# Cumulative logs of the gates kept in DRAM by batch and head instead of by tile

## What is computed

```python
log_f = jax.nn.log_sigmoid(x @ Wf.T + delta)
lf = jnp.cumsum(log_f.reshape(b, nc, C, H).transpose(1, 0, 3, 2), axis=-1)   # C = 128
def step(S, inputs):
    qb, kb, vb, lb = inputs
    o_inter = jnp.einsum('bhid,bhde->bhie', qb * jnp.exp(lb)[..., None], S)
    A = jnp.einsum('bhid,bhjd->bhij', qb, kb)
    diff = jnp.where(mask, lb[..., :, None] - lb[..., None, :], -jnp.inf)
    A = A * jnp.exp(diff)
    ...
```

## Time and profile before

| | |
|---|---|
| median of three runs | 893.77 us |
| profiled execution | 893.34 us |
| its span, first to last instruction | 891.6 us |
| TensorE matmul, busy | 800.4 us, 90% |
| DVE / ACT / GpSimd, busy | 566.5 / 498.7 / 429.0 us |
| mean granted TensorE clock | 0.952 of full |
| SP's DMA queue: packets, MB | 119904, 145.00 |
| all DMA | 132847 packets, 163.89 MB, mean 184 GB/s |

### The profile page before, as it was taken

One profiled execution on the slowest core, in us unless ns is written; L12 is line 12 of the kernel. 1 busy time (PEld: TensorE's weight loads), 2 busy tenths in 40 slices (PEclk: granted clock), 3 DMA queues, 4 the chain that ended last, 5 costly groups with the idle time before them and its releaser, 6 DMA issues.

```text
span 891.6 us, 15824 instructions
## 1 busy us (share of the span) xinstructions
PE 800.4 (90%) x5648; PEld 682.0 (76%) x5648; DVE 566.5 (64%) x1027; ACT 498.7 (56%) x1165; POOL 429.0 (48%) x383
## 2 busy tenths in 40 slices
PE   1665799999999999999999999999999999999930
PEld 1443578888888888888888888888888888888830
DVE  5685455657855775557665766568656766556575
ACT  4654755566546664665556645665566545654431
POOL 5647641656245642566255815563357525470230
PEclk9965699999999999999999999999999999999975
DMA  8756796658667775678576766676667767663947
GB/s 284 283 166 157 206 343 221 159 152 186 194 157 159 188 195 143 150 183 202 154 160 181 156 219 142 164 187 193 157 140 193 195 157 210 162 134 117 277 106 221
DMA packets 132847, 163.89 MB, mean 184 GB/s; under 512 B 11808, under 2 KB 102432, under 8 KB 132640
## 3 DMA queue, kind: packets, MB, share of 16 engines
q1 hardware_dynamic: 119904, 145.00, 55.6%
q0 software_dynamic: 12288, 16.79, 12.1%
q10 hardware_dynamic: 576, 1.09, 0.3%
HBM read 117.48 MB, written 45.35 MB: 183 GB/s over the span
## 4 chain that ended last, share of the span: by engine, by line
PE 64%; DVE 8%; POOL 7%; ACT 5%; issue 5%; DMA 5%; SPq 1%; another core or an unknown queue 1%; DVEq 0%; ACTq 0%; POOLq 0%
PE g_ps L1408 16%; PE y_ps L1434 15%; PE up_ps L1408 15%; PE a_ps L1374 3%; PE o_ps L1398 3%; DMA qk_dram<-qk_r 3%; PE m_ps L1326 3%; PE m_ps L1356 2%; POOL w_r L803 2%; PE m_ps L1334 2%; POOL ffn_dram L833 2%; PE m_ps L1351 1%; POOL xg L821 1%; DMA w_raw<-w_experts 1%; ACT dec_both L971 1%
## 5 line engine op out<-in xcount | busy, mean ns | idle before, releaser
L1434 PE MATMUL y_ps<-w_r,hid_r 128*128 128x256 f32 x1536 | 205.5, 283 | 1.6 <-DVE hid_r L1292 1.6
L1408 PE MATMUL up_ps<-xgt,w_r 128*128 128x512 f32 x768 | 203.8, 400 | 0.0
L1408 PE MATMUL g_ps<-xgt,w_r 128*128 128x512 f32 x768 | 201.6, 398 | 1.0 <-DVE sg L1278 1.0
L1434 PEld LDWEIGHTS y_ps<-w_r,hid_r 128*128 128x128 f32 x1536 | 192.9, 190 | 3.1 <-DVE hid_r L1292 2.3
L1278 DVE SCALAR_TENSOR_TENSOR sg<-sg,g_ps 128x512 f32<-128x512 f32 x128 | 87.6, 685 | 169.2 <-ACT sg L1062 162.5
L803 POOL TENSOR_TENSOR w_r<-w_raw,w_r 128x768 fp32r<-128x768 f32 x64 | 122.3, 1912 | 101.5 <-ACT w_r L991 101.2
L1408 PEld LDWEIGHTS up_ps<-xgt,w_r 128*128 128x128 f32 x768 | 138.2, 188 | 25.9
L1408 PEld LDWEIGHTS g_ps<-xgt,w_r 128*128 128x128 f32 x768 | 135.5, 189 | 24.2 <-DVE sg L1278 0.8
L1062 ACT ACTIVATE sg<-g_ps 128x512 f32<-128x512 f32 x128 | 76.4, 597 | 125.7 <-PE g_ps L1408 121.7
L833 POOL DMA_INDIRECT ffn_dram<-y_sb,idx_all x64 | 105.0, 1640 | 74.7 <-DVE y_sb L1206 58.9
L798 POOL TENSOR_SCALAR_AFFINE_SELECT lb_row<-lb_row 128x1024 f32<-128x1024 f32 x64 | 78.2, 1232 | 95.5 <-DMA lb_row<-lb_tiles 95.4
(11 more groups left out here) (234 smaller groups left out, 950.5 us busy)
## 6 DMA issues: line engine op xcount, KB each, us to landing
lb_row<-lb_tiles SPq DMA_DIRECT2D x64, 512.0 KB, 4.5
w_raw<-w_experts SPq DMA_DIRECT2D x64, 384.0 KB
qk_dram<-qk_r SPq DMA_DIRECT2D x32, 512.0 KB, 4.4
k_st<-qk_dram SPq DMA_DIRECT2D x96, 128.0 KB, 3.3
arena<-qk_dram SPq DMA_DIRECT2D x192, 64.0 KB, 3.4
x_all<-x SPq DMA_DIRECT2D x8, 512.0 KB, 10.3
xn_dram<-xn SPq DMA_DIRECT2D x8, 512.0 KB, 5.5
e_row<-lb_tiles SPq DMA_DIRECT2D x64, 64.0 KB
```

The source lines that it names most:

```text
L1408: mm = pe.matmul(bank[:, :], w_r[:, m, a, at:at + P], xgt[:, b, k, half * 512:(half + 1) * 512], start=(j == 0 and k == 0), stop=(j == len ...
L1434: mm = pe.matmul(y_ps[:, j, :], hid_r[p][:, a, j * P:(j + 1) * P], w_r[:, m, b, DOWN:DOWN + D], start=(m == 0 and q == 0 and j % 2 == 0), ...
```

## The change

The tensor becomes `lb_rows` [batch, head, tile of the batch, token] instead of `lb_tiles` [tile, head, token]. So the 512 tokens of a head in a batch lie in one piece of 2 KB, and the 8 heads of one tile lie 2 KB apart in pieces of 512 bytes, where they were one piece of 4 KB. `load_rows` reads the 4 tiles of 8 heads in one transfer (2 for 8 in each batch); `load_lb` keeps its one transfer; `store_lb` needs one for each batch (8 in all, 2 before), and the waits on `d_out` follow.

```diff
-    lb_tiles = nc.dram_tensor("lb_tiles", [NT, H, P], F32, kind="Internal").ap()
+    lb_rows = nc.dram_tensor("lb_rows", [B, H, TPB, P], F32, kind="Internal").ap()
...
                     for kk in range(KD):
-                        for c in range(TPB):
-                            sp.dma_start(e_row[:, kk, c * P:(c + 1) * P],
-                                         lb_tiles[b * TPB + c, kk * HH:(kk + 1) * HH, :].unsqueeze(1)
-                                         .broadcast_to([HH, HD, P])).then_inc(row_in, 16)
+                        sp.dma_start(e_row[:, kk, :], lb_rows[b, kk * HH:(kk + 1) * HH, :, :].rearrange("h c n -> h (c n)")
+                                     .unsqueeze(1).broadcast_to([HH, HD, N])).then_inc(row_in, 16)
 
                 def load_lb(n):
                     if n >= 2:
                         sp.wait_ge(e_done, 2 * n - 2)
-                    sp.dma_start(lb_row[n % 2][:, :, :], lb_tiles[n // 2, n % 2 * HH:(n % 2 + 1) * HH, :].unsqueeze(0)
+                    b, c = n // 2 // TPB, n // 2 % TPB
+                    sp.dma_start(lb_row[n % 2][:, :, :], lb_rows[b, n % 2 * HH:(n % 2 + 1) * HH, c, :].unsqueeze(0)
                                  .broadcast_to([P, HH, P])).then_inc(lb_in[n % 2], 16)
...
                 def store_lb(p):
                     sp.wait_ge(lb_turned, 2 * p + 2)
-                    sp.dma_start(lb_tiles.rearrange("(g t) h n -> (t h) g n", g=TPB)[:, GROUPS[p], :], lbt[p])\
-                      .then_inc(d_out, 16)
+                    for g in range(GROUPS[p].start, GROUPS[p].stop):
+                        for half in range(2):
+                            sp.dma_start(lb_rows[2 * g + half, :, :, :].rearrange("h c n -> c h n"),
+                                         lbt[p][half * TPB * H:(half + 1) * TPB * H, g - GROUPS[p].start, :])\
+                              .then_inc(d_out, 16)
...
-                sp.wait_ge(d_out, 16)
+                sp.wait_ge(d_out, 16 * 2)
...
-                        pool.wait_ge(d_out, 32)
+                        pool.wait_ge(d_out, 16 * B)
...
-                    act.wait_ge(row_in, 16 * KD * TPB * (b + 1))
+                    act.wait_ge(row_in, 16 * KD * (b + 1))
```

More of the change, by code:

```diff
@@ L108, in build @@
                   head_rows, delta_row, logits, turned, xt_stored, y_sb, attn_w, wo_r, arena, fixed)
-        mixed(nc, stage_of(makers), x, out, xn_dram, xt_dram, qk_dram, lb_tiles, s_dram, ffn_dram, w_experts, d_out,
+        mixed(nc, stage_of(makers), x, out, xn_dram, xt_dram, qk_dram, lb_rows, s_dram, ffn_dram, w_experts, d_out,
               ident, tri, ones, head_rows, delta_row, logits, qs0, qs1, e_row, xg, small, y_sb, xt_stored, dec_more, aff_t, top_val, top_at,
@@ L449, in top_step, with mixed @@
         dve.match_replace(aff_t[:, :], top_val[:, at], aff_t[:, :], -1.0).then_inc(topk, 1)
-def mixed(nc, stage, x, out, xn_dram, xt_dram, qk_dram, lb_tiles, s_dram, ffn_dram, w_experts, d_out, ident, tri, ones,
+def mixed(nc, stage, x, out, xn_dram, xt_dram, qk_dram, lb_rows, s_dram, ffn_dram, w_experts, d_out, ident, tri, ones,
           head_rows, delta_row, logits, qs0, qs1, e_row, xg, small, y_sb, xt_stored, dec_more, aff_t, top_val, top_at, neg_lb, exp_rest, exp_tot,
```

## The result

The changed kernel took 897.06 us (median of 11 runs, 10 of them between 895.2 and 899.3) beside 893.86 us for the kernel before, measured with it: ratio 1.004, interval 1.0029 to 1.0051, so +3.2 us. A second measurement (the tenth experiment) gave 897.18 beside 892.86, ratio 1.0053 (1.0038 to 1.0068). The change makes the kernel slower by 0.4 to 0.5%, at or just over the 0.3% that the prediction took as the bound of no change.

What follows compares the result with a forecast made beforehand. TensorE, busy 90% of the span, was taken as the bound, with transfers setting the end only before 141 us. Start +1.6 us, SP's time, stores and steady part zero: 893.34 + 1.6 = 894.9, 895.4 against the median; range 890.5 to 901.

Steps and rivals of the forecast that it cites:

- The packets: SP's DMA queue: some 170400 packets for 119904, and its share up by some 4 points.
- The start: To about 141 us: `lb_row` loads delay two weight loads and a `qk_dram` store by 0.50, 0.10, 1.00: +1.6 us.
- A load costs 0.50 us more: Each `lb_row` load at a full queue: 1.76 us in 512-byte pieces for 1.26 in 4 KB pieces.
- the upper bound of +1.46: Most an `lb_row` load could cost more, if it ran at 193 GB/s like the q loads: 2.72 us.
- The dear packet: Rival, 20%: `lb_row` loads run like q loads at 193 GB/s; +5.6 us at the start, nothing per batch, 899.4 us.
- SP's time: SP's issues: fewer `e_row` issues free 3.7 us per batch, hidden by waiting for GpSimd's weight halves; cost zero.
- That rival: 14%: SP's freed time at 68.11 us shortens the chain's wait at 80.09 us; 891.6 or 889.5 us.
- The stores: Stores of the logs, eight for two: some 0.4 us delay and 2.6 us of SP, both covered; zero.
- The steady part: After about 141 us: 3.6 us more queue time per batch, hidden by slack; zero, period still 95.1 us.
- both places that the prediction named: Steady part: second `qk_dram` store with 3.2 us of slack, mask of `lb_row` with 3.7; both hide the added cost.
- the rival of the tight place: 6%: loads costing over 3.2 us more make the second `qk_dram` store late in seven batches; some 920 us.
- No price at all: Rival, 10%: short pieces run as fast as long ones, or the compiler joins them; -0.5 to 0, 893.5 us.

Runs made afterwards that it cites:

- the tenth experiment: The changed kernel, unaltered, run again on one chip with the kernel before and three variants: 897.18 us, ratio 1.0053.
- the seventh experiment: The changed kernel with `e_row` read in eight transfers again, from the new layout: 896.39 us, ratio 1.0062 to the kernel before.
- the rows alone: Kernel before with both layouts stored; `e_row` read in two transfers from the new one, `lb_row` in 4 KB pieces from the old: 891.84 us, 0.9995.
- The experiment with eight loads of 64: Kernel before with logs stored twice; only the first eight `lb_row` loads read 512-byte pieces 2 KB apart: 896.96 us, ratio 1.0056.
- the burst: Kernel before with logs stored twice, 48 loads appended, short pieces at several distances: 281 GB/s at 1 KB, 171 at 2, 289 at 2.5, 71 at 4.
- the first burst: Kernel before with logs stored twice, 48 loads appended in six forms: old `lb_row` 387 GB/s, new 140, each partition's own 512-byte pieces 291.
- The padded change: The changed kernel with its rows 2.5 KB apart instead of 2 KB: 894.56 us, ratio 1.0017 to the kernel before.
- the padded pieces alone: Kernel before with logs stored twice; `lb_row` loads read 512-byte pieces 2.5 KB apart, `e_row` untouched: 893.14 us, ratio 1.0003.
- both copies: Kernel before with logs also stored in 512-byte pieces 2 KB apart, which no load reads; the control for later runs: 891.74 us, 0.9993.
- the 4 KB kernel: The changed kernel with its rows 4 KB apart instead of 2 KB: 945.11 us, ratio 1.0596 to the kernel before.
- the later 56 loads: Kernel before with logs stored twice; `lb_row` loads from the ninth on read 512-byte pieces 2 KB apart: 894.22 us, ratio 1.0024.

## Why the prediction held, and where it was off

**The time.** 895.4 us was forecast and 897.06 measured, inside the range of 890.5 to 901, 1.7 us over the number and just past the bound between no change (0.51) and slower (0.39). The forecast's mechanism, dearer packets on the chain at the start and cover in the steady part, is what the runs show; its sizes were off. That the time came so near is in part luck: the price of a load was far too low, and counting four loads in full was too high. With the measured 2.4 us a load, the forecast's own sum gives 4 x 2.4 - 0.4 = +9.2 us, where 3.2 and 4.3 were measured.

**The packets.** 170720 for the forecast 170400, and the share 5 points up for 4. The difference lies in the closing packets, taken as 16 for each transfer. The counts say otherwise: the seventh experiment, with `e_row` in 8 transfers again, moves 177248 packets, 6528 more than the change. Of them 6144 are pieces, so 48 transfers bring 384, 8 each. In the same way the eight stores of the new layout bring 4 each: the rows alone move 113920 packets, which is 119904 - 6144 - 384 + 512 + 32. The two old stores close with 32 together as well (the second copy adds 544 packets, 512 of them pieces), so the exact sum is 119904 + 57344 - 6144 - 384 = 170720.

**The start.** The term was +1.6 us, measured +3.96 in one trace and, in the other, 148.50 against 146.89, +1.6; that the second agrees to the tenth is chance, by the spread of the gate groups above. In the first, though no finer than that spread, 0.89 us stand against the 0.60 of the two weight loads, and 2.31 against the 1.00 of the place of the store. The times say +3.2 and +4.3 for the whole kernel. The experiment with eight loads of 64 puts the loss there: +0.56% for them, +0.58% for all.

**The step that failed is the price of a load.** "A load costs 0.50 us more" came from 388 to 390 us, 137 GB/s at a share of 0.46. Those pieces lie side by side in DRAM, where the new ones lie 2 KB apart, and their transfers came one every 0.62 us from SP, so the row held neither the distance nor a full queue. Measured with both, the load costs 3.74 - 1.35 = 2.4 us more, above even the upper bound of +1.46. That bound was taken from the q loads, whose 2 KB lie between one partition and the next, and that distance cost nothing in the burst (281 GB/s for the 291 of own pieces in the first burst). The prediction had named the stride as what speaks for the dear packet, and had put against it that q goes to 16 partitions. The runs don't bear this argument out: of the two 2 KB patterns it is the one read by all partitions alike, with the distance inside what each reads, that is costly. With the padding the load costs 0.46 us more, nearly the 0.50 of the forecast. The forecast's price of a short packet was right; the price of the distance was missing. The padded change stands at +1.7 us (894.56 against 892.86) beside the forecast's +1.6, but the padded pieces alone, four of the same loads at the start, stand at +0.3 (interval -0.6 to +1.3) where the forecast's counting gives 4 x 0.46 = 1.8. So that agreement doesn't confirm the counting.

That the loss isn't four times 2.4 us has its reason in the chain: parts of the loads lie under waits that were there anyway, such as the 12.41 us for `qk_dram`, 9.50 now. (3.96 + 0.40) / 4 gives 1.1 us per load for the four of the sum, by the larger of the two traces.

**The way to the chain** was another than forecast in part. Lengthened transfers of 0.5, 0.1 and 1.0 us on the same three places were named; in the trace the `lb_row` load of 107.56 us itself stands on the chain for 7.94 us, through GpSimd's mask, and at 127.63 us SP is held for 6 us in an issue of `ffn_dram`, ahead of the store at 134.16. Holding alone needn't cost: the padded pieces alone have the same 6.5 us at 125.06 us and lose nothing. The store that follows is issued at 131.60 and lands in 8.09 us, so from the first `ffn_dram` issue to the landing it takes 14.63 us, for 13.72 in before and 16.03 in the change. The queue is full either way; what counts is how fast it empties.

```profile
125.06 6.50 SPq L751 DMA_DIRECT2D ffn_dram<-y_sb  x2
131.60 4.20 SPq L668 DMA_DIRECT2D qk_dram<-qk_r  x2
```

**SP's time** at zero was right as far as the runs tell. The freed issues at 68.11 us went into held issues of `k_st` behind them, and the wait at 80 us stayed at 5.89 us for 5.85. That rival is refuted twice, by this wait and by the rows alone at 0.9995.

**The stores** at zero were right: both copies 0.9993, rows alone 0.9995.

**The steady part** at zero was nearly right: six periods lost 0.7 us together. The slack of the mask shrank from 3.7 to 2.0 us, and both places that the prediction named held. In the 4 KB kernel the rival of the tight place came true: forecast at 4.5 us more per load were 17.6 us at the start and 9 in the batches, and that kernel lost 18.9 at the start and 4.7 x 6 = 28 in six batches at 6.0 us more per load, with ACT's waits for weights among them, which the rival didn't name.

**The dear packet** (20%, 899.4 us) was right on its price being higher, and even so too high in time, as it counted all four loads in full. No price at all is refuted by each kernel with the pieces 2 KB apart. The prediction's estimate from the Trainium skill (DMA: Bandwidth & Descriptors, section Why small descriptors are slow) has a slip on which nothing else rests: with 0.20 us a load and the 0.17 us that `e_row` saves by the same rule the sum is +0.6, not +0.5.

**What stays open.** The 2 us of the later 56 loads in the times have no place in a trace. The padded change loses 0.17% and the padded pieces alone 0.03%; the rows alone lose nothing, so their sum falls short of the whole by about a tenth of a per cent, which is what these intervals can just tell. In the two traces `lb_row` at 106 us lands later in the padded change (8.55 us for 6.14), right behind the two big `e_row` transfers. But the rows alone show such a delay too, 7.34 us for 5.28 in the control, and lose nothing, so it isn't enough by itself. Open as well is whether own pieces 2 KB apart within a partition are slow.

## What to carry to other kernels

Take the price of a transfer from a row with the same pattern of addresses, not only the same size of piece, and from a stretch where the queue is full: where the DMA share is well under 1 and the issues stand back to back, the rate is that of the issuing engine. A share well under 1 can also be the mark of such a bad distance, so look at the rate and at SP's issues beside it. Where all partitions read the same data from DRAM, keep the pieces long, or keep the distance between them off 2 and 4 KB: 512 bytes of padding brought back two thirds of the loss here. Fewer issues are worth something only where the issuing engine's time ends a wait; here 3.7 us of SP per batch bought nothing that shows.

## What was not expected of the hardware

Short pieces that all 128 partitions read alike came at 281 GB/s with a distance of 1 KB, at 140 (from another tensor 153 over the group) with 2 KB, at 289 with 2.5 KB and at 71 with 4 KB, at first with the DMA engines idle for a third to two thirds of the time and, late in the 4 KB group, with a share of 1.03 at 78 GB/s. Pieces of 256 bytes at 1 KB came at 147. In the kernel the step from 2 to 4 KB cost 48 us, with the same packets and bytes.

An issue on SP isn't a fixed 0.4 to 0.6 us. Behind transfers of 1024 packets each an issue took 3.6 us and those of two stores of 512 KB 6.5, so SP's program stands still in them, with everything that is queued behind on SP.
